# Layer 2's edge pass: ScalarE copies gathered rows to eight buffers that TensorE reads

## What is computed

```python
def _L2_gnn_ref(x, edge_src, edge_dst, adj_vals, w_nbr, w_own, bias):
    h = x @ w_nbr
    msgs = adj_vals[:, None] * h[edge_src]
    agg = jax.ops.segment_sum(msgs, edge_dst, num_segments=x.shape[0])
    return agg + x @ w_own + bias
...
h = jnp.maximum(_layernorm(x, axis=-1), 0.0)
x = x + _L2_gnn_ref(h, src, dst, edge_weight, ...)
```

## Time and profile before

| | |
|---|---|
| median of three runs | 7474.96 us (7470.9 to 7496.99) |
| profiled execution | 7510.36 us, span of its core 7508.6 us |
| mean granted TensorE clock | 0.776 |
| layer 2's edge pass within the span | 3757 to 5044 us |
| busy over the span | PE 5223.0, DVE 4737.4, POOL 3882.0, ACT 2083.1 us |

### The profile page before, as it was taken

How to read it: one execution, slowest core, us unless ns; L and a number is a source line. 1 busy time by engine, 2 the same in 40 slices (tenths; PEclk the granted TensorE clock), 3 DMA queues, 4 the chain that set the end, 5 groups by cost and what they waited for, 6 DMA issues and landing times. The chain is left out here.

```text
span 7508.6 us, 80305 instructions
## 1 busy us (share of the span) xinstructions
PE 5223.0 (70%) x19641; PEld 3547.1 (47%) x19641; DVE 4737.4 (63%) x10520; ACT 2083.1 (28%) x5870; POOL 3882.0 (52%) x5290
## 2 busy tenths in 40 slices
PE   3899999996566666766655555547466666666567
PEld 2544444444455555555433333334355555455366
DVE  5799999995355555555644444447366656566765
ACT  2588888883210000101200000001011111111233
POOL 3455555550556655555466666662555555555010
PEclk9899999998766766767767676769666666667788
DMA  5322222223322322222233333332222222222201
GB/s 179 94 85 85 85 85 85 84 84 118 93 76 81 81 80 79 80 80 73 73 92 91 91 90 90 91 116 62 71 77 76 76 75 77 76 75 78 64 17 35
DMA packets 333404, 619.09 MB, mean 82 GB/s; under 512 B 95560, under 2 KB 208636, under 8 KB 332562
## 3 DMA queue, kind: packets, MB, share of 16 engines
q0 software_dynamic: 171200, 474.81, 22.6%
q1 hardware_dynamic: 148172, 126.47, 5.6%
q10 hardware_dynamic: 13616, 13.11, 0.5%
HBM read 553.77 MB, written 67.57 MB: 83 GB/s over the span
## 5 line engine op out<-in xcount | busy, mean ns | idle before, releaser
L290 POOL DMA_INDIRECT G<-table,ib x1760 | 1706.7, 970 | 429.1 <-issue 423.5
L548 PE MATMUL pM<-G,one 128*128 128x260 f32 (+1 forms) x3520 | 1291.5, 509 | 733.4 <-issue 394.6
L423 DVE TENSOR_TENSOR acc<-acc,pM 128x260 f32 (+1 forms) x1760 | 759.4, 431 | 1116.7 <-PE pM L548 466.2
L548 PEld LDWEIGHTS pM<-G,one 128*128 128x128 f32 x3520 | 792.4, 248 | 1071.1 <-issue 493.3
L1323 POOL DMA_INDIRECT G<-table,srcI x880 | 834.3, 948 | 633.4 <-ACT zt L1347 587.4
L655 PE MATMUL pM<-G,one 128*128 128x256 f32 x1760 | 665.8, 516 | 581.9 <-DVE one L628 432.6
L193 POOL DMA_INDIRECT G<-table,ib x880 | 845.0, 960 | 234.9 <-issue 233.0
L1447 PE MATMUL pM<-zt,one 128*128 128x512 f32 x1760 | 935.9, 613 | 4.6 <-DVE acc L1408 2.5
L1347 ACT ACTIVATE zt<-G,a4S 128x128 f32<-128x128 f32 x2640 | 857.0, 390 | 0.0
L469 ACT ACTIVATE oneT<-pT 128x512 f32<-128x512 f32 x440 | 261.6, 597 | 2030.2 <-PE pT L534 1144.3
L655 PEld LDWEIGHTS pM<-G,one 128*128 128x128 f32 x1760 | 387.0, 247 | 852.9 <-DVE one L628 586.2
(11 more groups left out here) (310 smaller groups left out, 7157.5 us busy)
## 6 DMA issues: line engine op xcount, KB each, us to landing
G<-table,ib POOLq DMA_INDIRECT x2640
far<-step_rec SPq DMA_DIRECT2D x224, 64.0 KB
G<-table,srcI POOLq DMA_INDIRECT x880
table<-row SPq DMA_DIRECT2D x100, 128.0 KB
table<-row SPq DMA_DIRECT2D x50, 132.0 KB
table<-row SPq DMA_DIRECT2D x50, 130.0 KB
base<-aux SPq DMA_DIRECT2D x50, 128.0 KB
bs<-base SPq DMA_DIRECT2D x50, 128.0 KB
```

Of the source, the lines that this page charges most:

```text
L290: pool.indirect_dma_start(G[:, par * C + j, 0:ROW], None, tab, bass.IndirectOffsetOnAxis(ap=ib[:, par * C + j:par * C + j + 1], axis=0)).t ...
L423: nc.vector.tensor_tensor(to, to, pM[j % R][:, :], ALU.add).then_inc(s_acc, 1)
L548: nc.tensor.matmul(pM[j % R][:, :], one[:, par * C + j, :], G[:, par * C + j, :], start=True, stop=True).then_inc(s_m, 1)
```

## The change

Eight buffers `row` of 128x256 floats and a semaphore s_row are added. ACT gets a copy per step: it waits for gather k, then until matmul k - 8 is done so that `row[k % 8]` is free, and copies `G[k % 16]` to `row[k % 8]`, counting s_row. PE waits for s_row instead of the gather and reads `row` in place of `G`. ACT's index copies are gated by s_row where they were gated by s_m: G is free once it is copied. DVE and POOL keep their instructions, and POOL its G buffers, sixteen as before.

```diff
--- before.py
+++ after.py
@@ -598,6 +598,9 @@
                 pM = [se.ps(f"pM{j}", [P, D]) for j in range(R)]
                 pO = [se.ps(f"pO{j}", [P, D]) for j in range(2)]
                 w_sb = se.sb("w_sb", [P, 2, D])
+                RC = 8
+                row = [se.sb(f"row{j}", [P, D]) for j in range(RC)]
+                s_row = se.sem("s_row")
                 s_w, s_o = se.sem("s_w"), se.sem("s_o")
                 EVERY = K // NT
 
@@ -617,7 +620,11 @@
 
                     @block.scalar
                     def _(act):
-                        steps(act, u, (0, gather_indices(act, u, u // 2, ib, s_ib, s_m, s_gt)))
+                        def copied(k, j):
+                            gathered(act, u, s_g, k, j)
+                            freed(act, s_m, k - RC + 1)
+                            nc.scalar.activation(row[j % RC][:, :], G[j][:, :], ACT.Copy).then_inc(s_row, 1)
+                        steps(act, u, (0, gather_indices(act, u, u // 2, ib, s_ib, s_row, s_gt)), (0, copied))
 
                     @block.vector
                     def _(dve):
@@ -650,9 +657,9 @@
 
                         def scatter(k, j):
                             pe.wait_ge(s_one, k + 1)
-                            gathered(pe, u, s_g, k, j)
+                            pe.wait_ge(s_row, k + 1)
                             freed(pe, s_acc, added(k - R))
-                            nc.tensor.matmul(pM[j % R][:, :], one[j % R][:, :], G[j][:, :], start=True, stop=True).then_inc(s_m, 1)
+                            nc.tensor.matmul(pM[j % R][:, :], one[j % R][:, :], row[j % RC][:, :], start=True, stop=True).then_inc(s_m, 1)
                             n = own_at(k)
                             if n is not None:
                                 freed(pe, s_acc, added(EVERY * (n - 1) - 1) + 1 if n >= 2 else 0)
```

## The result

| | before | after |
|---|---|---|
| time, median | 7475.52 us (7467.08 to 7499.64) | 7510.06 us (7491.08 to 7524.83) |
| profiled execution | 7510.36 us, span 7508.6 | 7509.63 us, span 7507.9 |
| layer 2's pass in it, first gather to last add | 1291.9 us | 1307.3 us |

The ratio is 1.0042, 95% interval 1.0031 to 1.0054, and the medians lie 34.5 us apart (0.46%). The two profiled executions happen to be equally long, since that of before took longer than any of its ten timed runs. So the loss has to be sought in the pass and not in the spans, and even the passes of these two differ by 15.4 us only; passes that follow one another in one execution, further down, give 28.8 and 33.9.

A forecast was written before the change was run, and what follows sets the result against it. It took layer 2's pass to be bound by POOL's gathers plus pauses while PE's counts arrive late; 7510.36 + 1 + 0 = 7511 profiled, or 7474.96 + 1 = 7476 us on the median's scale, own range 7440 to 7510.

The forecast's parts named there:

- rival C: Index copies queue behind ACT's row copies, lengthening each POOL pause: +38 to +76 us, 7525; chance 0.23 with DVE/PE slowdown included.
- What bounds the kernel: Layer 2's edge pass: POOL without index waits needs 1127 us of 1287; up to 154 us could come back.
- (1): 880 ScalarE copies in layer 2's pass, 416 ns each, 366 us in all, hidden in ACT's idle time: cost 0.
- (2): Copy added between gather and matmul: 0.4 to 0.5 us once at the start, perhaps again at the tail; +1 us.
- (3): Index copies wait for s_row instead of s_m, so gathers can be issued four steps further ahead of PE.
- (4): PE waits for s_row instead of the DMA's semaphore and reads `row`: one wait for one, cost 0.
- (5): Four steps more gather depth: POOL runs on 5 us longer, PE is held 5 us longer, pauses stay; 0 us.
- rival A: POOL's pauses vanish, being buffer shortage or PE reading freshly gathered tiles: up to -154 us, taken as -135, 7340; chance 0.18.
- the moment of the release: Sign in layer 2's timeline: PE's counts reach their waiters bunched, only once POOL has stopped issuing gathers.
- Rival B: Four steps more backlog lengthen pause cycles from 16 to 20 steps, 55 pauses become 44: -31 us, 7450; chance 0.15.

The follow-up runs named there:

- row4: Layer 2's pass ten times in one execution, pausing chip: before 1288.0 and 1287.9 us, changed 1320.2 and 1323.4, every block copied twice (pass 4) 1349.7.
- row3: Layer 2's pass nine times in one execution, free chip: before 1124.8 us, changed 1128.4, every block copied twice 1124.8, without gathers 635.2.

## Why the prediction was right and where it was wrong

The forecast was 7476, the time 7510.06 and before 7475.52. It is within 0.5% of before, as the forecast had it, and inside 7340 to 7550. But it lies just past the end of the forecast's own range (7440 to 7510), and the mechanism that moved it is rival C's. The forecast said that nothing but 1 us changes; that the real loss stayed below half a per cent was luck and no part of the reasoning.

- *What bounds the kernel.* Right: the pass lasts 1127 us where POOL doesn't wait, measured at 1125 to 1127 on free chips. I had found how much could come back, but not that it depends on the chip. My reading of rows 5 left out a part: between 4405.72 and 4416.98 DVE adds twice, at 4407.17 and 4410.75, and PE does one more step at 4408.06. The add of the step that ended at 4405.72 starts at 4418.25, so the "some 11 us" to the release hold.
- *(1) Copies: 416 ns each, cost 0.* The size holds (414). "Hidden" holds on a free chip, doubled or not. On a pausing chip it failed, and this is the step that went wrong: the gate's wait for the index copy grew by 33 of the 34 us, some 26 of them between release and resumption, where the copies stand. I had asked whether the copies keep up with DVE in a burst, the wrong test; the right one is what else stands in that queue, and I had named it in rival C. The Trainium skill (ScalarE: Activation LUTs, What ACT_TABLE_LOAD costs) gives 186 ns + 0.833 ns per element, 399 ns for this shape, and an overlap of about 93 ns between two that follow each other. The traces agree with both: 414 ns in the mean with waits between the copies, 401 for a copy right behind another (row4, pass 4), and there each starts 0.31 us after the one before it. In the timeline of after above the index copy starts at 3955.05, 0.09 us before the row copy of 3954.72 has ended.
- *(2) One link at the start, +1 us.* The first matmul starts 3.5 us after the first gather, before 3.0: 0.5 us. Right.
- *(3) Gathers run four steps further.* Right in the mechanism: 13 to 14 steps ahead at the resumption, 10 before.
- *(4) The swapped wait.* PE waits 33.0 us for copies by the view of waits above, which I had put at the start alone. That part of the forecast was wrong. Those waits can't have cost much beyond the pauses: in row4 the gate's idle time grew by 33.0 us of the 33.9 us that the change costs, so 0.9 us are left for them, for the start and for all else.
- *(5) Depth gives 0.* Right, and the part that decided against rival A: 32 buffers +9.0 us, four row buffers the same as eight.
- *Rival A* fell on all counts on pausing chips: neither buffers nor the operand matter. Against it I had the moment of the release, which held. The Trainium skill (Perfetto Trace Analysis, Identifying Performance Opportunities) says that a gap which repeats on the engine that should be saturated can mean too few buffers. Here it didn't: on a pausing chip 16 more of them left the gap (+9.0 us).
- *Rival B* fell: the pauses stayed 16 steps apart. The fewer waits in the view of waits were a matter of names.
- *Rival C* had the right mechanism, 0.7 us more per pause in 55 pauses, +38 to +76. Measured: 0.5 to 0.6 us, 29 to 34 us in the pass. It was mis-sized twice: I took a copy in the queue at 0.42 to 0.50 us, and copies that follow each other start 0.31 us apart, so the added stretch is 0.48 us and not 0.7; and I added a longer hold on top. Its bound "past 3.5 us with the number near 55" was met in row4 (3.60 and 3.89) and missed in the profile of after (3.31).

What decided between forecast and C was a term that I had worked out, 38 us, and then outweighed by an argument without a number ("PE works off its backlog during those 0.7 us"). PE did start as many steps behind a release as before, and the pause was longer all the same.

## What to carry to other kernels

An operation on an idle engine isn't free when that engine is also a link of the path that ends a stall: look at what is first in its queue at the moment of release, and price the new work there once per stall. Count stalls from the instructions of the engine that stalls, not from the waits that carry a name. And before a stall is explained, run the kernel before on another chip: here a seventh of its time was there on some chips and not on others.

## What the runs showed of the hardware that I had not expected

- Two kinds of chip. The same kernel before took 7463 to 7559 us on three chips of the experiments and 6413 to 6417 on four. The granted clock of the pass is 0.70 on both (first windows of row3 and row4), and the free chip isn't quicker in the pass without gathers (635.2 and 634.6 us).
- On the one kind, TensorE's counts reach their waiters late while GpSimd issues gathers without a break, in the earlier trace rows some 11 us after the modelled end of the matmul. Pauses of 1.75 us after each four gathers prevent it, a fill of 0.30 us does so in part (the gate waits 114.5 us in place of 160.4). It depends neither on the tile that TensorE reads, nor on the number of its reports, nor on written-out or looped code.
- 1760 activations of 128x256 in the pass, 655 us of ScalarE's time, moved nothing on a free chip (1124.8 and 1124.8), neither VectorE's adds nor the gathers. Two such activations that follow each other overlap by 0.09 us.
